# Radial features of a tensor-product layer laid by column pairs on 16 partitions

## The reference

```
x = silu(edge_radial @ W1 + b1)          # 8 -> 64
x = silu(x @ W2 + b2)                    # 64 -> 64
tpw = x @ W3 + b3                        # 64 -> 256, four 8x8 matrices an edge
m0 = ALPHA * (einsum('eu,euw->ew', hs_e * sh0, W00) + INV_SQRT3 * einsum('eui,ei,euw->ew', hv_e, sh1, W110))
m1 = ALPHA * (einsum('eu,ei,euw->ewi', hs_e, sh1, W01) + einsum('eui,euw->ewi', hv_e * sh0, W10))
agg = segment_sum(concat(m0, m1), dst) / sqrt(16)
```

## Time and profile before

| | |
|---|---|
| timed runs, us | 12874.27 (median), 12865.76, 12892.65 |
| profiled execution, us | 12867.33, its span 12865.4 |
| granted TensorE clock, mean of the span | 0.638 |
| window 6700 to 9230 us (tensor stage), busy us | PE 1842.15, DVE 1814.59, ACT 522.48, POOL 1476.50 of 2530 |

### The profile page before, as it was taken

The page is one execution under the profiler, slowest core; times in us unless marked ns, Lnnn a source line. Parts: engine busy times, 40 slices in busy tenths (PEclk is TensorE's granted clock), DMA queues, the critical chain, the costliest instruction groups (busy, mean ns, idle before and its releaser), DMA issues. The chain is left out here.

```text
span 12865.4 us, 86012 instructions
## 1 busy us (share of the span) xinstructions
PE 5229.5 (41%) x25371; PEld 3057.0 (24%) x25371; DVE 7050.3 (55%) x11102; ACT 3858.4 (30%) x6150; POOL 7257.5 (56%) x7431
## 2 busy tenths in 40 slices
PE   2225300038135555555537777777514343400001
PEld 1214300012134444444423222222211111100001
DVE  4754588888442222222227777677515555567761
ACT  0002333345023333333312222222102333356640
POOL 5645677748554444444456655555563555566654
PEclk5556655569556666666657777777657666655555
DMA  6101366634300000000011111111110111133331
GB/s 237 46 20 40 129 216 213 214 141 157 109 18 16 17 17 15 17 17 17 15 31 24 25 23 23 23 24 23 20 16 4 46 30 31 33 93 126 123 102 39
DMA packets 464212, 813.80 MB, mean 63 GB/s; under 512 B 227109, under 2 KB 324822, under 8 KB 413446
## 3 DMA queue, kind: packets, MB, share of 16 engines
q10 hardware_dynamic: 81456, 446.55, 8.9%
q0 software_dynamic: 234304, 156.53, 7.0%
q1 hardware_dynamic: 147990, 205.22, 4.9%
HBM read 401.53 MB, written 406.14 MB: 63 GB/s over the span
## 5 line engine op out<-in xcount | busy, mean ns | idle before, releaser
L1627 POOL DMA_INDIRECT hs<-tab_h,src_i x3136 | 2973.0, 948 | 2764.7 <-issue 1224.2
L1218 POOL DMA_INDIRECT en<-tab_s,src_i x1568 | 1571.0, 1002 | 827.8 <-issue 493.6
L1110 DVE SCALAR_TENSOR_TENSOR picked<-rank_ps,hot_hi 128x98 f32<-128x98 f32 x1568 | 313.3, 256 | 2106.2 <-remote 1146.8
L1912 PE MATMUL tp_ps<-w_pair,x 128*128 128x512 f32 x1568 | 1075.1, 774 | 435.4 <-DVE prod_b L2050 377.6
L2332 POOL DMA_INDIRECT rows_src<-out_rows,pos x784 | 754.2, 962 | 775.8 <-ACT out_rows L2378 503.2
L2357 PE MATMUL late_ps<-hot_col,hot_row 128*128 128x512 bf16 x1248 | 590.9, 486 | 1097.0 <-DVE hot_col L2456 670.0
L2456 DVE TENSOR_SCALAR hot_col<-count_up,pos_late 128x784 bf16<-128x784 f32 x624 | 628.1, 1030 | 726.8 <-remote 576.7
L2344 POOL DMA_INDIRECT hs<-tab_h,ptr x784 | 743.0, 948 | 367.1 <-issue 256.0
L1011 PE MATMUL rank_ps<-place_sb,hot_t 128*128 128x98 f32 x3136 | 868.6, 394 | 0.0
L2047 DVE TENSOR_TENSOR prod_a<-tp_ps,zz 128x768 f32<-128x768 f32 x392 | 374.7, 956 | 701.2 <-remote 478.6
L1011 PEld LDWEIGHTS rank_ps<-place_sb,hot_t 128*128 128x128 f32 x3136 | 705.5, 277 | 3.3
(11 more groups left out here) (408 smaller groups left out, 16290.9 us busy)
## 6 DMA issues: line engine op xcount, KB each, us to landing
sums<-rows ACTq DMA_DIRECT2D x98, 1088.0 KB
sums<-rows ACTq DMA_DIRECT2D x147, 512.0 KB
ev_rows<-zeros ACTq DMA_DIRECT2D x16, 3136.0 KB
raw<-ev_rows ACTq DMA_DIRECT2D x49, 1024.0 KB
r<-in_edge_attr_2x ACTq DMA_DIRECT2D x49, 1024.0 KB
y_rows<-r ACTq DMA_DIRECT2D x49, 1024.0 KB
y<-y_rows SPq DMA_DIRECT2D x49, 1024.0 KB
hs<-tab_h,src_i POOLq DMA_INDIRECT x3136
```

The lines of the kernel that those rows point to most:

```text
L1110: nc.vector.scalar_tensor_tensor(self.picked[:, g, :], self.rank_ps[q % 2][:, g, :], 1.0, self.hot_hi[k][:, at, :], ALU.mult, ALU.mult, ac ...
L1218: pool.indirect_dma_start(en[s][:, g, :], None, tab_s0, bass.IndirectOffsetOnAxis(ap=src_i[:, p * 2 * CH + g:p * 2 * CH + g + 1], axis=0)) ...
L1627: pool.indirect_dma_start(rows[k][:, g, :], None, tab_h, bass.IndirectOffsetOnAxis(ap=src_i[:, t * CH + g:t * CH + g + 1], axis=0)).then_i ...
L1912: nc.tensor.matmul(o, x2[k][:, a, b * EP:(b + 1) * EP], w3_cols, start=True, stop=False)
```

## The change

In the host's layout of the input, edge_attr_8 becomes, for each chunk, 16 partitions (2 columns x 8 features) by 8 column pairs by 128 edges, in place of 128 partitions by 128 edges. So w1_pair is one block of 16 x 128, the same for every pair of columns, and one product can stream 4 pairs x 128 edges = 512 columns. Hidden layer 1 of a chunk is then two such products with K = 16, not eight of 128 columns with K = 128. The sizes of the results are as before.

```diff
-        w1 = sb(weights, "w1_pairs", [128, CH // 2, 128])
+        w1 = sb(weights, "w1_pair", [2 * MUL, 128])
...
-            small = [(w1[n * MUL:(n + 1) * MUL, n // 2, (n % 2) * HID:(n % 2 + 1) * HID], A["L2_gnn_W1"]) for n in range(CH)]
+            small = [(w1[n * MUL:(n + 1) * MUL, n * HID:(n + 1) * HID], A["L2_gnn_W1"]) for n in range(2)]
...
-                for w in (w1[:, :, :], w2[:, :], w3_in[:, :, :], own_w[:, :]):
+                for w in (w1[:, :], w2[:, :], w3_in[:, :, :], own_w[:, :]):
                     nc.vector.memset(w, 0.0).then_inc(blank, 1)
...
-            radial_t = [sb(st, f"radial_t{s}", [128, 2, EP]) for s in range(2)]
+            radial_t = [sb(st, f"radial_t{s}", [2 * MUL, 2, CH // 2, EP]) for s in range(2)]
...
-                    sp.dma_start(radial_t[s][:, :, :], A["edge_attr_8"][2 * i:2 * i + 2, :, :].rearrange("k q p -> q k p")).then_inc(radial_in[s], 16)
+                    sp.dma_start(radial_t[s][:, :, :, :], A["edge_attr_8"][2 * i:2 * i + 2, :, :, :].rearrange("k q n p -> q k n p")).then_inc(radial_in[s], 16)
...
                 def hidden1(t, a):
                     u, i = layer1_at(t, a), t // 2
                     K.wait(pe, "pe", radial_in[i % 2], 16 * (i // 2) + 16, acted, u - 2)
-                    for b in range(4):
-                        last = nc.tensor.matmul(hid_ps[:, u % 3, b * EP:(b + 1) * EP], w1[:, a * 4 + b, :], radial_t[i % 2][:, t % 2, :], start=True, stop=True)
-                    return last
+                    four = radial_t[i % 2][:, t % 2, 4 * a:4 * a + 4, :].rearrange("q n p -> q (n p)")
+                    return nc.tensor.matmul(hid_ps[:, u % 3, 0:4 * EP], w1[:, :], four, start=True, stop=True)
...
-            a = _np.ascontiguousarray(a.reshape(EP, 2 * PAIRS, CH * 8).transpose(1, 2, 0))
+            a = _np.ascontiguousarray(a.reshape(EP, 2 * PAIRS, CH // 2, 16).transpose(1, 3, 2, 0))
```

## The result

The changed kernel takes 12,832.5 us, the median of 20 runs (12,801 to 12,871), against 12,874.1 before (20 runs, 12,845 to 12,915): a ratio of 0.9965, 95% interval 0.9955 to 0.9976, 41.6 us faster. The profiled execution shows about half of that: its span against the earlier trace rows is 19.5 us shorter.

A forecast was written before the change was run, and what follows sets the result against it. The prediction took the tensor stage to be paced by TensorE's semaphores, late while GpSimd issues gathers. Its -19 us there and -5 us from the weights gave -24 us, about 12,850 us, range 12,740 to 12,965.

The forecast's parts named there:

- Sum: Whole kernel: -19 us in the tensor stage and -5 us from the earlier stage's weights, -24 us in all.
- Hidden layer 1's streaming at nothing: TensorE in the tensor stage: the same 1,024 columns a chunk in fewer, longer products cost nothing.
- The backlog by records: Tensor stage: gather bursts tolerate some TensorE instructions, then delay each further one; 24 fewer take product 3 from 5.3 us late to on time.
- joined chunk: Tensor-stage chunk whose gather burst follows without pause: product 1's 16.1 us lateness goes, product 2 or 3 pays; 29.3 us.
- Loading radial_t at nothing: SP's 49 loads for the tensor stage, now onto 16 partitions: no cost, hidden by a lead of over 40 us.
- The pair of 21.2 and 29.3 us: Tensor stage: an on-time chunk of 21.2 us, then a joined one of 29.3; 25.3 a chunk against 25.5, -19 us.
- Slower rival: Tensor stage: on-time chunks beget joined bursts, each chunk costing 26.3 to 27.0 us; 12,985 us in all; chance 0.15.
- Late semaphores vanish: Tensor stage: 64 records a chunk stay below what bursts tolerate, GpSimd becomes the bound; 12,400 to 12,580 us; chance 0.10.
- Loads on the path: TensorE's weight loads paid beside the matmuls: 12 fewer save 1.4 us a chunk, to some 12,735 us; chance 0.05.
- Time, not records: Tensor stage: lateness goes by how long GpSimd has been gathering; stage unchanged, only -5 us, 12,869 us; chance 0.15.
- Weights in the earlier stage: SP issues 2 loads of layer 1's weights, not 16, shortening the DVE wait: -5 us, between 0 and -5.5.

The follow-up runs named there:

- e7: Changed kernel with 4 gathers a chunk, not 16, from the tensor stage's third chunk on; chip 8: 12,437.4 us, 0.9654 of the kernel before.
- e8: Kernel before the change with 4 gathers a chunk, not 16, from the tensor stage's third chunk on; chip 8: 12,356.4 us, ratio 0.9595.
- e1: Changed kernel with the weight loads and memsets of before, so only the tensor stage is changed; chip 10: 9,878.7 us, 1.0087 of the kernel before.
- e3: Changed kernel with hidden layer 1's two 512-column products on all 128 partitions, padded with zeros; chip 10: 9,786.5 us, 0.9996 of the kernel before.
- e2r: Changed kernel with hidden layer 1 again as eight products of 128 columns, on 16 partitions; chip 0: 12,937.9 us, 1.0008 of the kernel before.
- e3r: Changed kernel with hidden layer 1's two 512-column products on all 128 partitions, padded with zeros; chip 0: 12,995.6 us, 1.0051 of the kernel before.
- a1_after: Changed kernel, unedited, as a control on chip 0: 12,885.7 us, 0.9962 of the kernel before.
- e4r: Changed kernel with hidden layer 1 of chunk t + 2 moved ahead of product 2; chip 8: 12,909.5 us, 1.0020 of the kernel before.
- e2: Changed kernel with hidden layer 1 again as eight products of 128 columns, on 16 partitions; chip 10: 9,860.6 us, 1.0073 of the kernel before.
- e4: Changed kernel with hidden layer 1 of chunk t + 2 moved ahead of product 2; chip 10: 9,780.5 us, 0.9989 of the kernel before.

## Why the prediction was right, and where not

**Sum.** Forecast -24 us, measured -41.6 (on chip 5 -16, on chip 0 -50). The direction and range held, and for the stage as a whole so did the mean: 25.3 us a chunk forecast, 25.38 in the trace, 25.50 before. In the traces the stage's 96 chunks give 12 us (forecast 19) and the weights 10.6 (forecast 5); where the rest of the medians' 41.6 us lies, no trace tells. That the direction held is in part luck: the forecast knew nothing of a chip like chip 10, on which the estimate is 84 us slower.

**Hidden layer 1's streaming at nothing**: right for the columns, 3.62 us at half clock against 3.78 before. Missed was what those records do to the clock of those behind them. I had named the clock at the end as a thing that could shift products 2 and 3 by "up to a microsecond or two each", and gave it no term; it is 1.0 us a chunk where nothing else limits (e7 against e8, e1 against e3).

**The backlog by records**: right in that records count. Late and waited-for product 3 went from 64 chunks to 18, and e2r brings it back with records alone. That a burst tolerates a fixed number of them stays a reading: e3r has product 3 late more often than a1_after with the same number. In the joined chunk product 1 was to lose its 16.1 us of lateness. In long chunks behind short ones the median of it went from 16.1 us (15 chunks) to 7.5 (18 chunks), and that of product 3 rose from 3.7 to 11.4.

**Loading radial_t at nothing**: right. The first wait is 35.1 us against 33.9, and no later load is waited for.

**The pair of 21.2 and 29.3 us**: both terms were mis-sized, and both measured means lie outside the bounds given for them (20.5 and 32.7). A short chunk takes 19.1 us and a long one 33.5, a pair of 52.6 that costs more than two ordinary ones of before. But pairs are not the rule: half of the chunks (49) are neither, 23.4 us each, since TensorE at half clock ends product 3 late by itself, which leaves GpSimd a pause between bursts (4.00 us in chunk 31). That the mean came out at 25.3 is two errors that offset each other.

**Slower rival** (on-time chunks beget joined bursts): its mechanism is right, 18 of 19 short chunks are followed by a long one, and its price of 26.3 to 27.0 us is about what e3r and e4r pay (26.34 and 26.25). The prediction called chunks 48 and 49 the only such pair that the trace of before has to offer. That was misread: the same trace has 16 short chunks, 15 of them followed by a long one. The changed kernel mostly escapes it because product 3 ends late in its ordinary chunks, at half clock behind hidden layer 1; in e4r, whose clock is as low (0.71), nothing stands between products 2 and 3, product 3 ends sooner (a median of 9.8 us after the first gather of a burst that began after a pause, and 13.4 in the changed kernel), and the price is paid. **Late semaphores vanish** was seen only on chip 10 or with 4 gathers. **Loads on the path** fell by e2 against e1; 24 records more cost e2r 0.30 us a chunk, where this rival has 1.4 us for the 12 loads alone. **Time, not records** fell by e2r, and by the trace of the changed kernel itself, whose product 3 ends later in the burst and is seen at once.

**Weights in the earlier stage**: forecast -5, at most -5.5. On chip 10 it is 4.7. On the others the term was mis-sized: the instruction runs 10.6 us sooner in the first pair of traces and its wait is 8.4 us shorter in the pair of chip 5, since the 24 loads behind are through sooner as well. Why they are stays open. (The prediction calls the instruction L1769 once; it is L1770 in both kernels.)

So the gain on the chips with late semaphores is some 50 us from fewer records (e2r against a1_after, on chip 0) and some 10 from the loads, against a loss by the clock that these chips seem to hide in part behind late semaphores; that last part was not measured by itself. What decides how late a semaphore comes, and why chip 10 has none late with the same program, stays open: no run here tells. Left open too is a version good on both: e3 and e4 were level with before or just under it on chip 10 and slower on the others, and a pause in GpSimd's bursts, which they point to, wasn't tried.

## To carry over

Where an engine waits for a semaphore, compare its start with the end of what it waited for, chunk by chunk: a mean wait of 6.8 us in the changed kernel hid three kinds of chunks of 19, 23 and 33 us, and what shortens one kind can make more of another. A product on few partitions streamed no slower here (3.62 against 3.78 us), but where the product ahead of it ran at half clock, the one behind it did so too (69 chunks of 70, and 2 of 91 with the full 128 partitions). On chip 10 this was rarer where it had been moved into idle time. And a gain of half a per cent that rests on such a balance belongs to the chip it was measured on: the same edit may be worth -0.4% on one and an estimated +0.9% on another.

## What was unexpected

- The same program takes 12,870 to 12,935 us in the first result and on chips 0, 5 and 8, and 9,790 us on chip 10. In the tensor stage an estimate of the difference is 490 us of 3,080 (25.5 us a chunk with late semaphores against the 20.4 of e3 and e4 on chip 10, where the kernel before has no trace); the rest lies in other stages and wasn't looked into.
- The kernel with the faster TensorE was the slower one: granted clock 0.75 in place of 0.70, 110 us longer (e3r against a1_after).
- Zeros on 112 partitions raised the granted clock of the stage from 0.76 to 0.87 (e1 against e3), and so did placing the 16-partition product ahead of product 2 (0.85, e4).
